# Adapter kernel: slots of the first batches from the sort's eight largest keys, the table wanted from batch 3 on, transfers of W begun on other queues

## The reference

```python
h = einsum('bsh,bhk->bsk', x, W_down[role]) + b_down[role]      # 1024 -> 512
h = gelu(h)
u = einsum('bsk,bkh->bsh', h, W_up[role]) + b_up[role]          # 512 -> 1024
y = x + u
out = layernorm(y) * gamma[role] + beta[role]
```

## Time and profile before

| | us |
|---|---|
| median of 3 runs (range) | 1444.43 (1442.76 to 1447.44) |
| the profiled execution: time | 1444.22 |
| the profiled execution: span | 1442.2 |
| TensorE busy | 1402.1 (97%) |
| VectorE busy | 1206.6 (84%) |
| ScalarE busy | 775.9 (54%) |
| GpSimd busy | 176.3 (12%) |

### The profile page before, as it was taken

The page is one execution under the profiler, slowest core; times in us unless marked ns, Lnnn a source line. Parts: engine busy times, 40 slices in busy tenths (PEclk is TensorE's granted clock), DMA queues, the critical chain, the costliest instruction groups (busy, mean ns, idle before and its releaser), DMA issues.

```text
span 1442.2 us, 32228 instructions
## 1 busy us (share of the span) xinstructions
PE 1402.1 (97%) x6150; PEld 1155.4 (80%) x6151; DVE 1206.6 (84%) x1451; ACT 775.9 (54%) x2055; POOL 176.3 (12%) x257
## 2 busy tenths in 40 slices
PE   4799999999999999999999999999999999999997
PEld 3678888888888888888888888888888888888885
DVE  4689888888888888888888888988888888888888
ACT  3355555555555555555555555555555555555555
POOL 6068600000000000000000047620000000000000
PEclk9999999999999999999999999999999999999998
DMA  7788866666665665665665788776666666566653
GB/s 189 223 225 233 231 192 189 205 188 187 201 195 182 205 194 182 196 200 183 197 198 184 210 246 242 220 207 201 183 197 200 184 196 199 184 193 201 187 191 137
DMA packets 210599, 286.86 MB, mean 199 GB/s; under 512 B 25297, under 2 KB 156370, under 8 KB 210578
## 3 DMA queue, kind: packets, MB, share of 16 engines
q1 hardware_dynamic: 203538, 269.58, 61.1%
q0 software_dynamic: 6400, 16.00, 4.7%
q10 hardware_dynamic: 640, 1.05, 0.3%
HBM read 185.86 MB, written 100.66 MB: 199 GB/s over the span
## 4 chain that ended last, share of the span: by engine, by line
PE 90%; DMA 2%; DVE 2%; DVEq 2%; issue 1%; ACT 1%; SPq 1%; ACTq 0%
PE p_down L901 15%; PE p_down L902 15%; PE p_down L903 15%; PE p_up L901 15%; PE p_up L902 15%; PE p_up L903 15%; DVEq L230 1%; DMA h_dram<-h 1%; DMA h_quad<-h_dram 1%; DVE row L708 0%; DMA row<-in_L_cond_W_down 0%; SPq L269 0%; DVE h L718 0%; DVE row L701 0%; DVE hT_lo L694 0%
## 5 line engine op out<-in xcount | busy, mean ns | idle before, releaser
L901 PE MATMUL p_down<-wd_hi,xT_hi 128*128 x1012 | 395.0, 390 | 15.1 <-DVE wd_lo L653 14.2
L901 PE MATMUL p_up<-wu_hi,hT_hi 128*128 x1008 | 394.1, 391 | 8.5 <-issue 4.5
L903 PE MATMUL p_down<-wd_hi,xT_lo 128*128 x1012 | 394.4, 390 | 0.0
L902 PE MATMUL p_down<-wd_lo,xT_hi 128*128 x1012 | 394.4, 390 | 0.0
L902 PE MATMUL p_up<-wu_lo,hT_hi 128*128 x1008 | 392.7, 390 | 0.0
L903 PE MATMUL p_up<-wu_hi,hT_lo 128*128 x1008 | 392.7, 390 | 0.0
L535 ACT ACTIVATE hT_hi<-p_hT 128x512 fp32r<-128x512 f32 x126 | 75.5, 600 | 404.7 <-DVE p_hT L688 401.6
L708 DVE SCALAR_TENSOR_TENSOR row<-p_up,row 128x1024 f32<-128x1024 f32 x126 | 154.3, 1224 | 150.3 <-PE p_up L903 138.3
L901 PEld LDWEIGHTS p_down<-wd_hi,xT_hi 128*128 128x128 f32 x1012 | 190.4, 188 | 56.5 <-issue 17.0
L901 PEld LDWEIGHTS p_up<-wu_hi,hT_hi 128*128 128x128 f32 x1008 | 189.6, 188 | 52.1 <-issue 12.9
L521 ACT ACTIVATE xT_hi<-xT_raw 128x1024 fp32r<-128x1024 f32 x125 | 132.8, 1062 | 173.8 <-PE p_down L903 124.3
(11 more groups left out here) (141 smaller groups left out, 947.6 us busy)
## 6 DMA issues: line engine op xcount, KB each, us to landing
x_quad<-in_x SPq DMA_DIRECT2D x512, 128.0 KB, 3.3
row<-in_x SPq DMA_DIRECT2D x126, 512.0 KB, 4.0
out<-row SPq DMA_DIRECT2D x126, 512.0 KB, 2.8
h_dram<-h SPq DMA_DIRECT2D x128, 256.0 KB, 3.8
h_quad<-h_dram SPq DMA_DIRECT2D x512, 64.0 KB, 1.9
w_raw<-in_L_cond_W_down POOLq DMA_DIRECT2D x64, 64.0 KB, 4.2
w_raw<-in_L_cond_W_up POOLq DMA_DIRECT2D x64, 64.0 KB, 3.8
row<-in_L_cond_W_up POOLq DMA_DIRECT2D x16, 128.0 KB, 4.3
```

The source lines that it names most:

```text
L901: pe.matmul(dst, a_hi, w_hi, start=first, stop=False)
L902: pe.matmul(dst, a_hi, w_lo, start=False, stop=False)
L903: return pe.matmul(dst, a_lo, w_hi, start=False, stop=last)
```

## The change

- `KEY_TOP` is 10 x 128 - 1 instead of 9 x 128 - 1, and the keys' shifts change (384 for role 2, or 128 when `FEW` applies; 256 or -256 for role 1), so that bit 7 of a key is the slot of its batch (0 or 1) and the low seven bits give its number. The clamping of roles and the term -256 x role are gone.
- `first_keys` is an integer tile (no cast), and a new tile `first_slots` = (key >> 7) & 1 is written behind `first_numbers`; `first_known` counts 2 when both are there.
- TensorE waits for `first_known` 2 instead of `rows_ready`, loads three slots, and computes `weights_at` and `when_split` in registers. It waits for `rows_ready` just ahead of `pipeline`, from batch 3 on.
- VectorE loads the slots of batches 0 and 1 behind `split_first(0)`, those of 2 and 3 behind `subtract_half(2, 0)`, and its wait for `rows_ready` stands behind `split_first(7)`. The bias addition of batch 0 stands behind batch 2's two half transposes and `subtract_half(2, 0)` instead of ahead of them.
- ScalarE: `gelu(0)` stands behind `round_half(2, 0)` instead of ahead of it.
- Piece 2 of W is issued by GpSimd at the very start, piece 3 by SP as before, pieces 4 and 5 by SP behind x of batch 2, pieces 6 and 7 by GpSimd. SP no longer waits for `rows_ready` ahead of x of batch 2. The load of role 2's `b_down` row by GpSimd stands in the middle of the table's steps.
- GpSimd's scratch lines lie in `w_raw` instead of `h_quad`, and it waits for `key_ready` ahead of them.

```diff
-    KEY_TOP = 9 * P - 1
+    KEY_TOP = 10 * P - 1
...
@@ SP
             for b in range(2):
                 load_quads(sp.value_load(first_numbers[0:1, b:b + 1], min_val=0, max_val=B - 1), b)
-            load_first(sp, FD - 2)
             load_first(sp, FD - 1)
             sp.wait_ge(numbers_ready, 1)
-            sp.wait_ge(rows_ready, 1)
             load_x(2)
+            for n in (FD, FD + 1):
+                sp.wait_ge(first_split, n - RING + 1)
+                load_first(sp, n)
@@ GpSimd
             pool.memset(opener[:, 0:2], 0.0).then_inc(pieces_split, 1)
+            load_first(pool, FD - 2)
...
+            pool.wait_ge(key_ready, 1)
             step(pool.tensor_scalar(past_gate, index_row[0:1, :], one(P_GATE), None, ALU.is_ge),
...
+            load_bias(R - 1, 0)
             step(pool.tensor_scalar(slot, slot, one(P_FLIP), one(P_FEW), ALU.mult, ALU.add),
...
-            pool.wait_ge(first_raw[FD - 2], raw_once)
-            load_bias(R - 1, 0)
-            for n in range(FD, FD + FU):
+            for n in range(FD + FU - 2, FD + FU):
                 pool.wait_ge(first_raw[n - 2], raw_once)
                 pool.wait_ge(first_split, n - RING + 1)
                 load_first(pool, n)
@@ ScalarE
+            round_half(2, 0)
             gelu(0)
-            round_half(2, 0)
@@ VectorE, the sort
-            chain(dve.tensor_scalar(clamped, role_row, 0, R - 1, ALU.max, ALU.min))
...
-            dve.scalar_tensor_tensor(key, clamped, -256.0, down_row, ALU.mult, ALU.add).then_inc(sort_step, 1)
...
+            chain(dve.tensor_scalar(one(ONE_SHIFT), one(ONE_SHIFT), -256.0, None, ALU.add))
+            chain(dve.scalar_tensor_tensor(key, is_one, one(ONE_SHIFT), down_row, ALU.mult, ALU.add))
...
             chain(dve.max(first_keys[:, :], key))
-            chain(dve.tensor_copy(first_ints[:, :], first_keys[:, :]))
-            dve.tensor_scalar(first_numbers[:, :], first_ints[:, :], P - 1, P - 1, ALU.bitwise_and,
+            dve.tensor_scalar(first_numbers[:, :], first_keys[:, :], P - 1, P - 1, ALU.bitwise_and,
                               ALU.bitwise_xor).then_inc(first_known, 1)
+            dve.tensor_scalar(first_slots[:, :], first_keys[:, :], 7, 1, ALU.logical_shift_right,
+                              ALU.bitwise_and).then_inc(first_known, 1)
@@ VectorE, the first batches
+            def first_slot(b):
+                at = dve.value_load(first_slots[0:1, b:b + 1], min_val=0, max_val=1)
+                return at * PARAMS, at * 16 + 16
+
+            params_at, when_loaded = [0] * 4, [0] * 4
             split_first(0)
+            dve.wait_ge(first_known, 2)
+            for b in range(2):
+                params_at[b], when_loaded[b] = first_slot(b)
...
             subtract_half(1, 1)
-            dve.wait_ge(rows_ready, 1)
-            params_at = [look_up(dve, PARAMS_AT, b, 0, PARAMS) for b in range(4)]
-            when_loaded = [look_up(dve, WHEN_LOADED, b, 16, 16 * R) for b in range(4)]
-            dve.wait_ge(bias_loaded, when_loaded[0])
-            bias_h(0, params_at[0], p_down[:, :])
             transpose_half(2, 0)
             transpose_half(2, 1)
             subtract_half(2, 0)
+            for b in range(2, 4):
+                params_at[b], when_loaded[b] = first_slot(b)
+            dve.wait_ge(bias_loaded, when_loaded[0])
+            bias_h(0, params_at[0], p_down[:, :])
             subtract_half(2, 1)
...
             split_first(7)
+            dve.wait_ge(rows_ready, 1)
@@ TensorE
-            pe.wait_ge(rows_ready, 1)
+            pe.wait_ge(first_known, 2)
...
-            weights_at = [look_up(pe, WEIGHTS_AT, b, 0, HC * K) for b in range(3)]
-            when_split = [look_up(pe, WHEN_SPLIT, b, 1, (R - 1) * (DN + UN) + 1) for b in range(3)]
+            slots = [pe.value_load(first_slots[0:1, b:b + 1], min_val=0, max_val=1) for b in range(3)]
+            weights_at = [n * (HC * K) for n in slots]
+            when_split = [n * (DN + UN) + 1 for n in slots]
...
             mm.then_inc(up_done, 2)
+            pe.wait_ge(rows_ready, 1)
             pipeline(pe, body, 3, B + 1)
```

More of the change, by code:

```diff
@@ L111, in adapter_kernel @@
         rank = sb("rank", [P, 1])
-        first_keys = sb("first_keys", [1, 8])
-        first_ints = sb("first_ints", [1, 8], I32)
+        first_keys = sb("first_keys", [1, 8], I32)
         first_numbers = sb("first_numbers", [1, 8], I32)
+        first_slots = sb("first_slots", [1, 8], I32)
         (N_FIRST, N_ONE, MOST, ONE_SHIFT, FEW, FIRST_SHIFT, P_FEW, P_MOST, P_ONE, P_OVER, P_REST, P_END, P_NA, P_GATE, P_FLIP,
@@ L122, in adapter_kernel @@
         down_row = w_raw[0][0:1, 3 * B:4 * B].bitcast(I32)
-        clamped, is_first, is_one, key = (w_raw[1][0:1, n * B:n * B + B] for n in range(4))
-        past_gate, past_mid, slot, step_of = (h_quad[0:1, n, 0:B] for n in range(4))
+        slot, is_first, is_one, key = (w_raw[1][0:1, n * B:n * B + B] for n in range(4))
+        past_gate, past_mid, step_of = is_first, is_one, w_raw[0][0:1, 3 * B:4 * B]
         p_down = psum("p_down", K)
@@ L356, in _, with load_bias @@
             pool.memset(opener[:, 0:2], 0.0).then_inc(pieces_split, 1)
+            load_first(pool, FD - 2)
+            def load_bias(role_at, at):
+                src = b_down[bass.ds(role_at, 1), :].rearrange("o k -> (o k)").partition_broadcast(P)
+                pool.dma_start(cols(params, at + BD, K), src).then_inc(bias_loaded, 16)
             done = [0]
@@ L406, in _ @@
                     ins.then_inc(rows_ready, 1)
-            def load_bias(role_at, at):
-                src = b_down[bass.ds(role_at, 1), :].rearrange("o k -> (o k)").partition_broadcast(P)
-                pool.dma_start(cols(params, at + BD, K), src).then_inc(bias_loaded, 16)
             def load_params(role_at, at, count):
@@ L624, in _ @@
             dve.wait_ge(roles_loaded, 16)
-            chain(dve.tensor_scalar(clamped, role_row, 0, R - 1, ALU.max, ALU.min))
-            dve.tensor_scalar(is_first, clamped, float(R - 1), None, ALU.is_equal, ALU.add,
-                              accum_out=one(N_FIRST)).then_inc(sort_step, 1)
-            dve.tensor_scalar(is_one, clamped, 1.0, None, ALU.is_equal, ALU.add, accum_out=one(N_ONE)).then_inc(sort_step, 1)
-            dve.scalar_tensor_tensor(key, clamped, -256.0, down_row, ALU.mult, ALU.add).then_inc(sort_step, 1)
-            steps[0] += 3
+            dve.tensor_scalar(is_first, role_row, R - 1, None, ALU.is_ge, ALU.add, accum_out=one(N_FIRST)).then_inc(sort_step, 1)
+            dve.tensor_scalar(is_one, role_row, 1, None, ALU.is_equal, ALU.add, accum_out=one(N_ONE)).then_inc(sort_step, 1)
+            steps[0] += 2
             dve.wait_ge(sort_step, steps[0])
-            dve.tensor_scalar(one(FEW), one(N_FIRST), float(B - 6), -384.0, ALU.is_ge, ALU.mult).then_inc(counted, 1)
+            dve.tensor_scalar(one(FEW), one(N_FIRST), float(B - 6), -256.0, ALU.is_ge, ALU.mult).then_inc(counted, 1)
             chain(dve.tensor_scalar(one(MOST), one(N_FIRST), float(10 - B), one(N_ONE), ALU.add, ALU.max))
@@ L635, in _ @@
             chain(dve.tensor_scalar(one(ONE_SHIFT), one(MOST), 4.0, 512.0, ALU.is_ge, ALU.mult),
-                  dve.tensor_scalar(one(FIRST_SHIFT), one(FEW), 1024.0, None, ALU.add))
-            chain(dve.scalar_tensor_tensor(key, is_one, one(ONE_SHIFT), key, ALU.mult, ALU.add))
+                  dve.tensor_scalar(one(FIRST_SHIFT), one(FEW), 384.0, None, ALU.add))
+            chain(dve.tensor_scalar(one(ONE_SHIFT), one(ONE_SHIFT), -256.0, None, ALU.add))
+            chain(dve.scalar_tensor_tensor(key, is_one, one(ONE_SHIFT), down_row, ALU.mult, ALU.add))
             dve.scalar_tensor_tensor(key, is_first, one(FIRST_SHIFT), key, ALU.mult, ALU.add).then_inc(key_ready, 1)
```

## The result

| | before | after |
|---|---|---|
| median (range), 6 runs each | 1446.57 (1442.76 to 1447.44) | 1438.53 (1437.75 to 1440.17) |
| ratio of the two, 95% interval | | 0.9951 [0.9938, 0.9964] |
| span of the profiled execution | 1442.2 | 1436.4 |

Faster by 0.49%, 7.1 us on 1446 (5.2 to 9.0 by the interval); the two medians lie 8.0 apart. Three more runs of before put its median at 1446.57: the execution on whose rows the prediction rests (1444.22) was at the quick end of its kernel.

The account below looks back on a forecast made before the run. It took the start-up chain ahead of batch 3 to set the end, with TensorE gapless afterwards; 8.7 + 1.1 = 9.8 us gained, less 0.8 for crowding, gave 9.0 and 1435.4 us, range 1432.5 to 1440.0.

Parts of the forecast that it names:

- forecast case: Whole kernel: 9.0 us gained, 1435.4 us, own range 1434 to 1436.8; chance 0.62.
- rival 1: Crowded start: piece 2 of W ahead of x costs 2.2 us, TensorE starts at 14.7, total 1437.6; chance 0.17.
- rival 2: Batch 0's h round trip through DRAM slows by 6.8 us, leaving 3.0 gained, total 1441.4; chance 0.08.
- What bounds, and one for one behind batch 19: TensorE without a gap at 10.88 us a step; shifts ahead of batch 3 move the end equally; splitting stretch counted 0.
- slower rival: Splitting of role 2's weights meets VectorE's work: 11.7 us lost against 9.0 gained, total 1446.9; chance 0.03.
- The profile's releaser was wrong, the table held TensorE: TensorE's first product waited for GpSimd's table and six look-ups, not W's fourth split; 8.7 us later than its data.
- Rival 3: W's fourth split really held TensorE: start only at 20.5, gain 1.8 us, total 1442.6; chance 0.03.
- Start 8.7 earlier: TensorE's first product starts at 12.5 instead of 21.20 us, once x's low part is there.
- Bias addition 9.8 earlier: Batch 0's bias addition on VectorE at 22.9 instead of 32.69 us: 8.7 from the start, 1.1 from look-ups.
- 0.8 for crowding: Loss of 0.8 us for x of batch 2, x of batch 0 and h together, from transfers in flight beside them.
- Behind: x's rows keep their distance: Past the start, splits 7 and 8, x's rows and parameters keep their distance to the chain: 0 in the splitting stretch.
- What the single parts bring: Gain at batch 0's bias addition: 8.7 us from TensorE's earlier start, 1.1 from VectorE's look-ups no longer ahead.

Follow-up runs that it names:

- tensor_only: Kernel before with only the new sort, the slots and TensorE's new wait and three loads; 1438.39 us, ratio 0.9944.
- old_transfers: Changed kernel with all transfers as before the change and SP again waiting for the table ahead of x of batch 2; 1441.56 us, ratio 0.9966.
- again: The changed kernel, unaltered, timed and profiled once more; 1438.69 us, ratio 0.9944 to the kernel before.
- piece2_sp: Changed kernel with piece 2 of W back on SP, behind x of batches 0 and 1; 1438.43 us, ratio 0.9946.
- best: Changed kernel with piece 2 on SP behind x, batch 0's bias addition ahead of batch 2's transposes, role 1's parameters behind x's second row; 1437.45 us, ratio 0.9942.
- te_ve_late_b_up: Changed kernel with old transfers, bias addition ahead of batch 2's transposes, role 2's b_up, gamma, beta held until h is read back; 1437.83 us, ratio 0.9944.

## Why the prediction was right, step by step

- *The number.* 1438.53 lies in the range of 1432.5 to 1440.0, but not in the forecast case's own 1434 to 1436.8; it stands between rival 1's 1437.6 and rival 2's 1441.4. Of the 3.1 us above 1435.4, 2.1 are before's median, which rose from 1444.43 to 1446.57, and 1.0 is gain that did not come. The mechanism was right, two terms of the sum were off (the start's 8.7 too large, crowding's 0.8 too small), and some of what made up for them was luck, as the steps show.
- *What bounds, and one for one behind batch 19.* Right: 10.88 a step again, and the gain at batch 19 (6.0) is the gain of the span (5.8). Over the other traces the two gains agree to 2.0 us. The stretch before it, 16 steps, lost 2.4 us before and 1.5 to 3.8 in the thirteen other traces; that is its own scatter, and the forecast's 0 for it stands. The slower rival's 11.7 was never near (its time, on the base of the other cases, is 1447.1 and not 1446.9).
- *The profile's releaser was wrong, the table held TensorE.* Right: tensor_only starts at 12.24 with the fourth split unmoved. Rival 3 is out.
- *Start 8.7 earlier.* 7.6 after, 7.2 and 7.6 in the repetitions. The term was mis-sized by rival 1's mechanism, at about half its price: piece 2 on GpSimd delays x by 1.0 to 1.6 us (11.29 to 11.54 against 9.92 to 10.28), not 2.2, and so takes back the 0.5 of x's earlier issue too, which was counted 0. The Trainium skill, DMA: Bandwidth & Descriptors, "Issuing engines are not separate DMA queues", had the sign: another issuer, the same 16 engines.
- *Bias addition 9.8 earlier.* 9.0, 7.7 and 8.5. Beside the later start it is the product's length, taken as 10.33 us from before: 9.88, 10.74 and 10.29, by how many of its first matmuls stand 0.43 apart. VectorE waits 1.25 to 1.5 us for the product in all three, so the new order behind batch 2's subtraction cost nothing, as taken; old_transfers shows the price, 5 us, once x of batch 2 comes late.
- *0.8 for crowding.* At the first up product 7.46, 7.08 and 7.15 us were gained where 9.8 less 0.8 was forecast, so 2.3 to 2.7 were lost: 1.1 to 1.5 at the start, 0.6 to 1.5 in the way, and up to 0.4 more or less by the product's length, which is not crowding. This is the term that was too small. The cause of the longer way is one of the two named: with `b_up` held back it is 9.3 to 9.5, which is 1.5 below before, and there pieces 6 and 7 are issued ahead of h as well. Rival 2's 6.8 was too much.
- *Behind: x's rows keep their distance.* Not in the first profile (2.3 lost between the up product and batch 3); in two repetitions the distance was 1.2 shorter than before instead, a gain at b3 of 8.3 and 8.4 of which that 1.2 stood in no term: luck, since it was before's profiled execution that had a late row. It scatters above a floor: 16.9 us from the up product to b3 in nine of the traces, 18.1 before. What makes one execution's rows late is open.
- *What the single parts bring* was left as a sum of 8.7 + 1.1. The runs put it differently: TensorE's wait and loads alone, with the new sort, have the whole gain that the times resolve (0.9944 against 0.9944). The other parts earn 1.7 to 2.1 us at the first up product in the traces, which the times could not show.
- *The signs.* Of those for right, batch 0's addition came as said (23.71). TensorE's start (13.60 for 12 to 13), the first up product (38.38 for 36.5), b3 (58.74 for 55), the gain at b19 (6.0 for 9) and the table (20.56 for 20) came late. Again's start of 14.02 touches the sign of rival 1. The sign of rival 2, over 8 us from the store of h to its last quad, was met: 25.09 to 36.11 is 11.0. But it was set wrong, since before already took 9.5 (34.07 to 43.57).

## What to carry to other kernels

A releaser in a profile is inferred from what ended last ahead of an instruction; ask the program's waits which one it needed, and try that one alone, since here it was all of the gain that the times resolve. When a start-up chain is shortened, everything that used to be ahead of its round trip through DRAM is now beside it: move the bulk transfers that are wanted late behind the round trip, not onto another queue. And use milestones of several traces: at 0.1 to 0.2% the times cannot rank variants that one milestone separates by 3 us.

## What the runs showed of the hardware that was not expected

- TensorE's granted clock fell from 1.00 to 0.50 (2.4 to 1.2 GHz) shortly behind gaps of 2.6 and 2.7 us between matmuls (piece2_sp, best) and was back after about 5 us of steady work; behind gaps of 2.1 to 2.5, and of 2.85 and 3.38 (te_ve_late_b_up, old_transfers), it did not fall.
- The first 6 to 14 matmuls of TensorE's first product, differing by the execution, stood 0.43 us apart and the rest 0.23; the clock column reads 1.00 for all of them, and the reason is open.
- Two executions of one program (after and again), with the same order of issues and those just ahead of the rows within 0.5 us, had 512 KB rows land in 9.5 and in 5.8 us. Whether they were on one chip is not on record.
